# Two side steps later: where TensorE turns the outputs of the recurrence during the first attention

## The chip, the cores and the metric

The kernel runs on one core of a Trainium2 chip. The metric is the device time of one execution in microseconds. Beside the runs that were only timed, one execution was recorded by the hardware profiler; all rows below are from it. Its engines are TensorE (PE; PEld is its weight load), VectorE (DVE), ScalarE (ACT), GpSimd (POOL) and SyncE (SP), which issues nearly all transfers.

## The reference, cut to what matters

A decoder of two layers works on 16 sequences of 128 tokens with 256 channels. In the first layer a causal attention with 16 heads is followed by a recurrence over the tokens, whose keys are the normalised residual and whose values are a context; its outputs are added to the residual, and a mixture of experts follows.

```python
x = x + _L0_attn_ref(_layernorm(x), W_Q, W_K, W_V, W_O, ...)
x = x + _L0_xattn_ref(16, 128, 256, time_decay, time_first, _layernorm(x), ctx_2048)
x = x + _L0_ffn_ref(_layernorm(x), router_w, ...)

# the recurrence, for each of 128 tokens
ww = u + kt
q = maximum(pp, ww)
e1, e2 = exp(pp - q), exp(ww - q)
y_t = (e1 * aa + e2 * vt) / (e1 * bb + e2)
```

## The kernel before, in words

Every engine has a program of its own, written out in Python, and the engines meet at semaphores only. An engine works through its instructions in order, so an instruction that waits holds all that is queued behind it on that engine.

The first attention is a loop of 64 steps `n`. Four steps make a stage `p` (one group `g` of four sequences and four heads), so a group takes 16 steps. In a step TensorE issues the scores (L732), turns the probabilities of two steps ago (L740), does three projections for the next stage (`fill`: six matmuls at L563 to L565 each, to bank 0 and bank 1 by turns), multiplies with the output weights (L759) and with the values (L749). VectorE takes the projected values out of their bank (L1625), copies the attention's output (L1646), adds to the residual (L1653), normalises probabilities (L1641), masks scores (L1631) and takes their maximum (L1634). A projection may not write bank 0 or bank 1 before the one that wrote it last has been taken out; for the values that is L1625.

While the attention of group `g` runs, the recurrence of group `g - 1` and the routing for it are woven in as side work. Side work is a Python generator, of which the loop runs one piece at each `side.step()`. TensorE has five such places in a step `n`: behind the scores, behind L740, behind the first projection, behind the second and behind the third. A `pause(k)` lets k of them go by. So the pauses alone decide between which instructions of the attention a piece of the side work stands.

The recurrence is done in two chunks for each group, `kt` 0 and 1, of 128 channels. For a chunk TensorE turns the normalised tiles into bank 5 (L575), ScalarE copies them out as keys, VectorE does the recurrence with scans (L1294 to L1332) with help of ScalarE and of GpSimd (L2648, L2649), TensorE turns the outputs `w_y` into bank 5 (L608, in `wkv_chunk`), and VectorE adds them to the residual (L1337). Bank 5 is the only bank of the side work: whoever writes it waits on `side_read` until the last content has been read. Six chunks, two each in groups 0 to 2, go through this function; the last group has one of its own (`last_group`).

GpSimd meanwhile splits the weights of the next stages in two parts (L2640, L2642). Each such split waits until the projections that read the old weights have been done.

Of the kernel before, what the change touches and what calls it, by code (L numbers as in the profile page):

```python
# [157 lines left out]
def pause(n):  # L158
    for _ in range(n):
        yield  # L160
# [30 lines left out]
def build(nc, io, out, phases=6):  # L191
    with ExitStack() as ctx:
# [365 lines left out]
        def tensor_program(pe):  # L558
# [13 lines left out]
            def turn_norm(i, kt, to):  # L572
                for b in range(GB):
                    pe.wait_ge(ln_norm, GB * i + b + 1)
                    m = T.transpose(to[:, b * P:(b + 1) * P], tiles_xn[i % 2][:, b, kt * P:(kt + 1) * P], ident[:, :])  # L575
                return m
# [22 lines left out]
            def wkv_chunk(c):  # L599
                g, kt = divmod(c, KT)  # L600
                use = SIDE["key", c]
                pe.wait_ge(side_read, use)
                turn_norm(NORM["wkv", g], kt, bank[5]).then_inc(side_filled, 1)
                yield from pause(15)
                pe.wait_ge(wkv_y, c + 1)
                pe.wait_ge(side_read, SIDE["y", c])
                for b in range(GB):
                    m = T.transpose(bank[5][:, b * P:(b + 1) * P], w_y[:, b, :], ident[:, :])  # L608
                m.then_inc(side_filled, 1)
                yield from pause(2)  # L610

            def wkv_group(g):
                yield from pause(5)
                for kt in range(KT):
                    yield from wkv_chunk(KT * g + kt)
# [2512 lines left out]
```

## Time and profile before

| What | Value |
|---|---|
| Median of 3 runs | 1897.95 us (1893.75 to 1899.11) |
| The profiled execution: its time | 1894.33 us |
| The profiled execution: its span | 1892.5 us |
| TensorE matmul busy | 1639.5 us, 87% of the span |
| VectorE busy | 1256.6 us, 66% |
| ScalarE busy | 877.7 us, 46% |
| GpSimd busy | 549.8 us, 29% |
| The six turns of outputs (L608) | from 247.3 us to 615.4 us |

The shares are averages over stages with different limits. What counts for one edit is the stretch around it: which instruction waits there, for whom, and who waits behind it.

### The profile page before, as it was taken

Reading aid. Unit: us, or ns where it says so; the run is one execution under the profiler, and the core shown is the slowest. Engines: PE = TensorE matmul, PEld = TensorE weight load, DVE = VectorE, ACT = ScalarE, POOL = GpSimd, SP = SyncE. Lnnn points to the kernel's source line nnn. Section 1 sums busy time; section 2 is a strip of 40 time slices with the busy share of each in tenths; the row PEclk is TensorE's granted clock in tenths of the full one; section 3 lists DMA queues with packets and bytes.
Section 4 is the critical chain, followed back from the end, with each engine's and each line's share of the span. In section 5 each row is a group of like instructions: output and inputs, shape, how many; then the busy total and the mean of one; then the engine's idle time right before and its main releaser. Section 6 shows DMA issues by size and latency. Waiting matters only on the chain. (4 is left out here: it accounts for less than half of the span.)

```text
span 1892.5 us, 25681 instructions
## 1 busy us (share of the span) xinstructions
PE 1639.5 (87%) x8566; PEld 1307.3 (69%) x8566; DVE 1256.6 (66%) x2677; ACT 877.7 (46%) x2528; POOL 549.8 (29%) x443
## 2 busy tenths in 40 slices
PE   6999979988997877799997688799878999999866
PEld 5878868776876655577775366577657887788644
DVE  4654786777688666454445556765656778877878
ACT  4534434434443444122222334555336666666666
POOL 2132331723352163300005654552123122211000
PEclk9999999988999898899998678899899999999989
DMA  7243433422352062233334110000100111000001
GB/s 262 68 137 120 160 99 112 169 95 95 130 190 98 28 178 68 73 106 106 107 93 141 34 34 23 23 1 1 45 24 28 39 41 41 12 1 1 1 1 45
DMA packets 82072, 143.37 MB, mean 76 GB/s; under 512 B 8981, under 2 KB 44437, under 8 KB 81813
## 3 DMA queue, kind: packets, MB, share of 16 engines
q1 hardware_dynamic: 75796, 124.94, 20.3%
q0 software_dynamic: 6144, 16.79, 2.7%
q8 instruction: 70, 1.15, 0.3%
q14 instruction: 62, 0.50, 0.1%
HBM read 86.90 MB, written 54.79 MB: 75 GB/s over the span
## 5 line engine op out<-in xcount | busy, mean ns | idle before, releaser
L2308 ACT ACTIVATE self_attention<-self_attention,small 128x128 f32<-128x128 f32 x256 | 99.9, 392 | 121.8 <-DVE small L1634 121.8
L2838 POOL TENSOR_TENSOR cross_attention_heads<-cross_attention_heads 128x512 f32<-128x512 f32 x64 | 70.4, 1100 | 285.2 <-DVE cross_attention_heads L1977 285.2
L2453 ACT ACTIVATE narrow_attention<-bank,small 128x128 f32<-128x128 f32 x256 | 90.4, 365 | 110.7 <-DVE small L1867 110.4
L759 PE MATMUL bank<-self_attention 128*128 128x256 f32 x512 | 130.4, 400 | 12.8 <-DVE residual L1653 12.8
L2537 ACT ACTIVATE cross_attention_heads<-cross_attention_heads,small 128x128 f32<-128x128 f32 x256 | 99.6, 390 | 90.2 <-DVE small L2001 90.2
L1103 PE MATMUL bank<-cross_attention,cross_attention_heads 128*128 128x256 f32 x512 | 124.8, 387 | 15.0 <-DVE residual L2015 10.1
L2704 POOL DMA_INDIRECT narrow_attention<-picked_outputs,dispatch x64 | 62.8, 981 | 235.4 <-DMA picked_outputs<-tiles 207.4
L563 PE MATMUL bank<-x_channel_major,qkv_weights_split 128*128 128x512 f32 x256 | 118.0, 461 | 6.6 <-DVE qkv_weights_split L1671 2.9
L759 PEld LDWEIGHTS bank<-self_attention 128*128 128x128 f32 x512 | 101.0, 201 | 32.3 <-DVE residual L1653 16.4
L1103 PEld LDWEIGHTS bank<-cross_attention,cross_attention_heads 128*128 128x128 f32 x512 | 95.5, 191 | 38.3 <-DVE residual L2015 22.3
L2640 POOL CAST qkv_weights_split<-self_attention 128x1024 fp32r<-128x1024 f32 x45 | 49.5, 1100 | 249.2 <-DMA self_attention<-in_wqkv 195.0
L2642 POOL TENSOR_TENSOR qkv_weights_split<-self_attention,qkv_weights_split 128x1024 fp32r<-128x1024 f32 x45 | 107.8, 2395 | 3.6
L857 PE MATMUL bank<-experts,tiles 128*128 x316 | 108.7, 467 | 0.0
L2316 ACT COPY self_attention<-bank 128x512 f32<-128x512 f32 x64 | 37.5, 585 | 143.2 <-PE bank L740 143.2
L564 PE MATMUL bank<-x_channel_major,qkv_weights_split 128*128 128x512 f32 x256 | 102.8, 401 | 0.0
L565 PE MATMUL bank<-x_channel_major,qkv_weights_split 128*128 128x512 f32 x256 | 102.5, 400 | 0.0
L1625 DVE TENSOR_TENSOR self_attention<-bank,self_attention 128x512 f32<-128x512 f32 x64 | 43.7, 684 | 84.8 <-PE bank L565 84.6
L959 PE MATMUL bank<-narrow_attention 128*128 128x16 f32 x512 | 70.2, 270 | 25.2 <-DVE narrow_attention L1872 14.2
L959 PEld LDWEIGHTS bank<-narrow_attention 128*128 128x128 f32 x512 | 69.5, 211 | 29.0 <-DVE narrow_attention L1872 28.6
L575 PE MATMUL bank<-identity,normalised_tiles 128*128 128x128 f32 x160 | 36.8, 337 | 58.9 <-DVE normalised_tiles L1237 35.6
L1077 PEld LDWEIGHTS bank<-cross_attention,cross_attention_heads 128*128 128x128 f32 x512 | 66.7, 192 | 27.0 <-issue 26.8
L1765 DVE TENSOR_TENSOR experts<-experts,bank 128x176 f32<-128x176 f32 x79 | 26.6, 337 | 87.1 <-ACT experts L2409 87.1
(382 smaller groups left out, 4735.6 us busy)
## 6 DMA issues: line engine op xcount, KB each, us to landing
picked_inputs<-self_attention SPq DMA_DIRECT2D x64, 512.0 KB, 6.2
self_attention<-in_wqkv SPq DMA_DIRECT2D x48, 512.0 KB, 6.1
experts_far<-picked_inputs SPq DMA_DIRECT2D x79, 128.0 KB, 2.0
picked_outputs<-tiles SPq DMA_DIRECT2D x79, 128.0 KB, 1.7
self_attention<-in_wo SPq DMA_DIRECT2D x16, 512.0 KB, 4.1
experts<-in_moe SPq DMA_DIRECT2D x4, 1408.0 KB, 13.8
self_attention<-in_bv SPq DMA_DIRECT2D x16, 256.0 KB, 5.3
bitnet_weights<-in_bitgu SPq DMA_DIRECT2D x8, 416.0 KB, 3.3
```

The source lines that it names most:

```text
L563: T.matmul(out_ap, w_hi, x_hi, start=first, stop=False)
L564: T.matmul(out_ap, w_hi, x_lo, start=False, stop=False)
L565: return T.matmul(out_ap, w_lo, x_hi, start=False, stop=last)
L759: m = T.matmul(bank[7][:, 0:D], ZT_a[n % 2][:, h, :], wo_a[p % 2][:, h, :], start=h == 0, stop=h == HG - 1)
L857: m = T.matmul(bank[2 + n % 2][:, 0:2 * EI].rearrange("p (m c) -> p m c", m=2), t_xT[n % 2][:, k, :], wup[:, :, k, bass.ds(at, EI)], start ...
L959: m = T.matmul(bank[6][:, hh * DS:(hh + 1) * DS], n_PT[n % 2][:, h, :], n_v[bb % 8][:, hh * DS:(hh + 1) * DS], start=True, stop=True)
L1103: m = T.matmul(bank[7][:, 0:D], ZT_x[n % 2][:, h, :], x_wo[hg % 2][:, h, :], start=h == 0, stop=h == HG - 1)
L2308: m = S.activation(P_a[u][:, h, :], P_a[u][:, h, :], ACT.Exp, bias=negmax_a[u][:, h:h + 1], accum_out=sums_a[u][:, h:h + 1])
L2453: m = S.activation(n_P[v][:, h, :], s4_in[:, h, :], ACT.Exp, bias=n_negmax[v][:, h:h + 1], accum_out=n_sums[bb % 2][:, q4 * 4 + h:q4 * 4 + ...
L2537: m = S.activation(P_x[u][:, h, :], P_x[u][:, h, :], ACT.Exp, bias=negmax_x[u][:, h:h + 1], accum_out=sums_x[u][:, h:h + 1])
L2642: G.tensor_tensor(wqkv[m][1], third(t), wqkv[m][0].bitcast(F32), ALU.subtract).then_inc(w_split, 1)
L2838: G.tensor_tensor(x_qsq, x_queries[f % 2], x_queries[f % 2], ALU.mult).then_inc(x_squared, 1)
```

## The change

The pause ahead of the turn of the outputs grows from 15 to 17 side steps, and the pause of two behind it goes. The steps of a chunk add up to the same number, so all that comes after keeps its place. No instruction is added or removed, and the other engines' programs are the same.

```diff
                 turn_norm(NORM["wkv", g], kt, bank[5]).then_inc(side_filled, 1)
-                yield from pause(15)
+                yield from pause(17)
                 pe.wait_ge(wkv_y, c + 1)
                 pe.wait_ge(side_read, SIDE["y", c])
                 for b in range(GB):
                     m = T.transpose(bank[5][:, b * P:(b + 1) * P], w_y[:, b, :], ident[:, :])
                 m.then_inc(side_filled, 1)
-                yield from pause(2)
+                yield from pause(0)
```

Two places on TensorE show it. The first is the first chunk of a group (`kt` 0). Before, the turn of the outputs (L608) stood between the scores and the turn of the probabilities:

```order
L732 MATMUL bank2<-self_attention 128x128 x4
L608 MATMUL bank5<-identity,wkv 128x128 x4
L740 MATMUL bank4<-identity,self_attention 128x128 x4
L563 MATMUL bank0<-x_channel_major,qkv_weights_split 128x512
L564 MATMUL bank0<-x_channel_major,qkv_weights_split 128x512
L565 MATMUL bank0<-x_channel_major,qkv_weights_split 128x512
L563 MATMUL bank0<-x_channel_major,qkv_weights_split 128x512
L564 MATMUL bank0<-x_channel_major,qkv_weights_split 128x512
L565 MATMUL bank0<-x_channel_major,qkv_weights_split 128x512
L575 MATMUL bank5<-identity,normalised_tiles 128x128 x4
```

Now it stands behind L740 and one projection, right ahead of the turn of the second chunk's keys (L575):

```order
L732 MATMUL bank2<-self_attention 128x128 x4
L740 MATMUL bank4<-identity,self_attention 128x128 x4
L563 MATMUL bank0<-x_channel_major,qkv_weights_split 128x512
L564 MATMUL bank0<-x_channel_major,qkv_weights_split 128x512
L565 MATMUL bank0<-x_channel_major,qkv_weights_split 128x512
L563 MATMUL bank0<-x_channel_major,qkv_weights_split 128x512
L564 MATMUL bank0<-x_channel_major,qkv_weights_split 128x512
L565 MATMUL bank0<-x_channel_major,qkv_weights_split 128x512
L608 MATMUL bank5<-identity,wkv 128x128 x4
L575 MATMUL bank5<-identity,normalised_tiles 128x128 x4
```

L608 writes bank 5 and L575 writes it again, so L575 waits for L1337, which reads it in between; nothing is left on TensorE to do between the two.

The second place is the second chunk of a group (`kt` 1), in the last step of a stage. Before, L608 stood behind the second projection of the step, the one to bank 1, and ahead of L759:

```order
L565 MATMUL bank1<-qkv_weights_split,x_channel_major 128x512
L608 MATMUL bank5<-identity,wkv 128x128 x4
L759 MATMUL bank7<-self_attention 128x256 x4
L563 MATMUL bank0<-qkv_weights_split,x_channel_major 128x512
L564 MATMUL bank0<-qkv_weights_split,x_channel_major 128x512
```

Now L759, the projection to bank 0, L749 and the last projection of the step, again to bank 1, all stand ahead of it:

```order
L565 MATMUL bank0<-qkv_weights_split,x_channel_major 128x512
L749 MATMUL bank6<-self_attention 128x128 x4
L563 MATMUL bank1<-qkv_weights_split,x_channel_major 128x512
L564 MATMUL bank1<-qkv_weights_split,x_channel_major 128x512
L565 MATMUL bank1<-qkv_weights_split,x_channel_major 128x512
L563 MATMUL bank1<-qkv_weights_split,x_channel_major 128x512
L564 MATMUL bank1<-qkv_weights_split,x_channel_major 128x512
L565 MATMUL bank1<-qkv_weights_split,x_channel_major 128x512
L608 MATMUL bank5<-identity,wkv 128x128 x4
L732 MATMUL bank2<-self_attention 128x128 x4
```

So L759, two projections of six matmuls each, and L749 pass L608.

## Rows read from the trace of the kernel before

**Rows 1.** Who waited for whom: engine, line, releaser; us, times, longest.

```profile
PE bank L608 <- DVE wkv L1332: 22.8, 3, 8.6
```

**Rows 2.** Timeline around the first chunk: start, duration, engine, instruction, idle before.

```profile
243.08 0.79 PE L563 MATMUL bank<-qkv_weights_split,x_channel_major 128*128 128x512 f32 x1 [4.90 <-DVE self_attention L1625]
...
245.80 1.91 PE L732 MATMUL bank<-self_attention 128*128 128x128 f32 x8
247.50 1.01 PE L608 MATMUL bank<-identity,wkv 128*128 128x128 f32 x4
...
252.14 0.66 PE L575 MATMUL bank<-identity,normalised_tiles 128*128 128x128 f32 x4 [1.79 <-DVE residual L1337]
```

**Rows 3.** Timeline of VectorE in the first group: add of chunk 0, then chunk 1.

```profile
251.41 0.68 DVE L1337 TENSOR_TENSOR residual<-bank,residual 128x512 f32<-128x512 f32 x1
...
280.77 0.41 DVE L1653 TENSOR_TENSOR residual<-bank,residual 128x256 f32<-128x256 f32 x1
...
286.20 0.68 DVE L1625 TENSOR_TENSOR self_attention<-bank,self_attention 128x512 f32<-128x512 f32 x1
287.48 0.69 DVE L1337 TENSOR_TENSOR residual<-bank,residual 128x512 f32<-128x512 f32 x1 [0.61 <-PE bank L608]
291.56 0.69 DVE L1625 TENSOR_TENSOR self_attention<-bank,self_attention 128x512 f32<-128x512 f32 x1 [3.39 <-PE bank L565]
...
295.60 2.39 DVE L1641 TENSOR_TENSOR self_attention<-self_attention,small 128x512 f32<-128x512 f32 x1
```

**Rows 4.** Timeline of VectorE at the second chunks of the groups after it.

```profile
445.82 0.41 DVE L1653 TENSOR_TENSOR residual<-bank,residual 128x256 f32<-128x256 f32 x1
...
451.24 0.68 DVE L1625 TENSOR_TENSOR self_attention<-bank,self_attention 128x512 f32<-128x512 f32 x1
...
457.68 0.69 DVE L1625 TENSOR_TENSOR self_attention<-bank,self_attention 128x512 f32<-128x512 f32 x1 [4.47 <-PE bank L565]
...
611.51 0.41 DVE L1653 TENSOR_TENSOR residual<-bank,residual 128x256 f32<-128x256 f32 x1
...
621.25 0.69 DVE L1625 TENSOR_TENSOR self_attention<-bank,self_attention 128x512 f32<-128x512 f32 x1 [4.70 <-PE bank L565]
```

**Rows 5.** Timeline of TensorE at the same two places.

```profile
451.38 1.11 PE L608 MATMUL bank<-identity,wkv 128*128 128x128 f32 x4 [8.58 <-DVE wkv L1332]
452.28 3.62 PE L759 MATMUL bank<-self_attention 128*128 128x256 f32 x8
...
458.29 0.48 PE L563 MATMUL bank<-qkv_weights_split,x_channel_major 128*128 128x512 f32 x1
...
459.76 1.05 PE L732 MATMUL bank<-self_attention 128*128 128x128 f32 x8
...
614.72 1.11 PE L608 MATMUL bank<-identity,wkv 128*128 128x128 f32 x4 [5.58 <-DVE wkv L1332]
615.62 3.62 PE L759 MATMUL bank<-self_attention 128*128 128x256 f32 x8
...
623.32 1.05 PE L732 MATMUL bank<-self_attention 128*128 128x128 f32 x8
```

**Rows 6.** Timeline of TensorE in the first group, after the second chunk.

```profile
296.38 1.89 PE L759 MATMUL bank<-self_attention 128*128 128x256 f32 x8
...
300.86 0.50 PE L563 MATMUL bank<-x_channel_major,qkv_weights_split 128*128 128x512 f32 x1 [0.31 <-ACT self_attention L2298]
```

**Rows 7.** Timeline of GpSimd there.

```profile
293.94 1.04 POOL L2640 CAST qkv_weights_split<-self_attention 128x1024 fp32r<-128x1024 f32 x1 [8.21 <-PE bank L565]
295.06 2.38 POOL L2642 TENSOR_TENSOR qkv_weights_split<-self_attention,qkv_weights_split 128x1024 fp32r<-128x1024 f32 x1
```

**Rows 8.** Two lines' instructions: duration ns min/median/max, first and last start.

```profile
L1641 DVE TENSOR_TENSOR self_attention<-self_attention,small x64: 691/692/2408, 44.2 to 648.7; 128x512 f32<-128x512 f32 x64
L1220 DVE BATCH_NORM_STATS2 small<-residual x96: 401/409/428, 4.5 to 1822.5; 128x6 f32<-128x256 f32 x96
```

**Rows 9.** Timeline of TensorE in a later stage, after a gap of another length.

```profile
756.40 1.60 PE L821 MATMUL bank<-identity,experts 128*128 128x128 f32 x8 [2.90 <-ACT experts L2388]
```

## The prediction

> **What bounds the kernel now.** I read the list of waits first, then the timelines of TensorE and VectorE around the six turns of the outputs, since the change touches nothing else. TensorE sits idle ahead of L608 in only three of the six chunks: 22.8 us in all, the longest 8.6 [rows 1]. These are the second chunks of the three groups; in the first chunks L608 starts at once behind L732 [rows 2]. The reader should see why those 8.6 us aren't all to be had. L608 waits for VectorE, and VectorE isn't idle while TensorE waits: it works in order through the recurrence and the attention's pieces, and its idle time around L608 is short before L1337 (0.61 us) and long behind it (3.39 us, waiting for a projection) [rows 3]. So in this stretch VectorE leads up to L1337; behind it TensorE leads for a moment, because it has been kept from its projections. What can be saved is what VectorE waits for these projections, less what it will wait for the later L608. The profiled execution took 1894.33 us, span 1892.5; the median of the three runs is 1897.95. I carry the difference over onto the median.
>
> **First chunks (three).** L608 goes behind L740 and a projection. The same instructions lie between L732 and L575, so they end when they ended before, 1.79 us before L575 started, at 250.35 [rows 2]. VectorE comes to L1337 only at 251.41, busy with its queue [rows 3]. L608 is therefore about 1.06 us early even in its new place, L1337 stays where it is, and so does L575 behind it. The other two groups show the same order of events. Cost 0, hidden by VectorE's queue. If that cover went, every microsecond of lateness would count on both engines, since L575 now has nothing ahead of it.
>
> **Second chunks (three).** TensorE no longer stops for the outputs. Next it is held by L759, which needs VectorE's L1653: its end is at 280.77 + 0.41 = 281.18, 445.82 + 0.41 = 446.23 and 611.51 + 0.41 = 611.92 [rows 3, 4]. From L759 to the end of the last projection TensorE took 459.76 - 452.28 = 7.48 us in the second group and 623.32 - 615.62 = 7.70 in the third, both begun after a long gap, at the lower clock (the eight matmuls of L759 took 3.62 us there and 1.89 in a busy stretch) [rows 5, 6]. I take these lengths, for the gap ahead of L759, though shorter, is still long: TensorE fell idle at 451.38 - 8.58 = 442.80 and 614.72 - 5.58 = 609.14 [rows 5], so 3.5 and 2.8 us. Inside the stretch the last projection needs bank 1, which L1625 frees at 286.20 + 0.68 = 286.88 and 451.24 + 0.68 = 451.92 [rows 3, 4]. It would start 7.48 - (459.76 - 458.29) = 6.01 us in, at 287.2 and 452.3, so this adds nothing. Then comes L608 at the full clock (0.66 us, the length of L575, four turns of the same size [rows 2]), then L1337 (0.69), then the L1625 that VectorE waited for before. With 0.03 us for the start of L759:
> - first group: 281.21 + 7.48 + 0.66 + 0.69 = 290.04, where it was 291.56: 1.5 us gained;
> - second: 446.26 + 7.48 + 0.66 + 0.69 = 455.09, was 457.68: 2.6 us;
> - third: 611.95 + 7.70 + 0.66 + 0.69 = 621.00, was 621.25: 0.25 us.
>
> **GpSimd's split.** The split of the weights waits for the last projection. It began at 293.94, as soon as that had ended, and its second half ran from 295.06 to 297.44 [rows 7]; L1641, which started in that time, took 2.39 us, while its median is 0.692 [rows 3, 8]. The last projection now ends at 281.21 + 7.48 = 288.69 instead, 5.25 us earlier, so the second half runs from 289.8 to 292.2, and L1641 comes at 295.60 - 1.52 = 294.1: clear of it, 1.70 us shorter. TensorE can't follow all the way. L759 at 296.38 stood 0.78 us behind L1641's start, up to which it can close; and the projection at 300.86 had 0.31 us idle [rows 6]. So of 1.70 us 1.09 counts. The second group has the same pattern; in the third nothing is left to split. That is 2 x 1.09 = 2.2 us.
>
> Here the Trainium skill has a rule that would turn this term round. What the rows show: L1641 is held, but L1220, the statistics of the normalisation, never is: 96 of them took 401 to 428 ns [rows 8]. In its new place the split runs while VectorE is at L1220. The Trainium skill, SBUF — State Buffer, calls the port pair of VectorE and GpSimd an exclusive lock for which the loser fully blocks, for VectorE's instructions with two SBUF inputs or in a two-port mode. L1641 agrees, and L1220 has a single input; had it such a mode, the split would hold it, and the sum would be that of the third rival. I go by the rows: the sum keeps this term.
>
> **Sum.** 0 + 1.5 + 2.6 + 0.25 + 2.2 = 6.5 us. 1894.3 becomes 1887.8, and on the median 1897.95 - 6.5 = 1891.4. I expect it to reach the end of the kernel, since what follows starts by semaphores, with no fixed time in it.
>
> **Bounds of the clock.** A gap of 2.90 us was followed by slow matmuls (1.60 us for eight turns) and one of 1.79 wasn't (0.66 for four) [rows 9, 2]. The new gap of the third group, 2.8 us, lies by the first, so I take slow. Were TensorE at full clock throughout, L759 to the last projection would take 300.86 - 0.31 - 296.38 = 4.17, and with 1.47 for the projection 5.64 us [rows 5, 6]. The third group would gain 7.70 - 5.64 = 2.1 us more; the first two are then held by L1625 at 286.88 and 451.92 and gain 0.3 each. Best case 6.5 + 2.7 = 9.2 us, or 10.4 if the whole 1.70 counts twice.
>
> **Rivals.**
> 1. *TensorE stays at the lower clock through the whole stretch* (slower). It now has two short gaps in place of one long, and does its work between. At that clock a projection takes 245.80 - 243.08 = 2.72 us, L732 and so L749 1.70, L608 1.01 [rows 2], L759 3.62 [rows 5]: with two projections and L1337 12.46 us from L759 on. That gives 293.7, 458.7 and 624.4, against 291.56, 457.68 and 621.25: 2.1 + 1.0 + 3.2 = 6.3 us lost, 1904.3. It decides where L759 to L608's end passes 291.56 - 281.21 - 0.69 = 9.7 us in the first group, instead of 8.14. Against it: after the single gap the last projection was at full speed, 1.47 us [rows 5].
> 2. *It is taken back later.* TensorE is 87% busy overall; if later pieces are TensorE's or the transfers' to set, an early VectorE only waits longer. Then 1897.95, with an even chance for either side of it. For it speaks that VectorE waited 3.39 and 4.47 us for projections [rows 3, 4]; against, that behind the chunk TensorE itself waits for VectorE and ScalarE [rows 6].
> 3. *The split moves onto L1220.* L1220 would stand still from about 290.7 to 292.2, 1.5 us in each of two groups. The sum would be 6.5 - 3.0 = 3.5 us, 1894.5. Its steady length speaks against it [rows 8].
> 4. *Full clock early*: 9.2 us, 1888.7.
>
> **How the numbers follow.** Forecast (gain of 4.5 to 8.5 us) 0.50, rival 4 0.12, rival 3 0.10, rival 2 0.20, rival 1 0.08. 0.3%, about what a measurement tells from no change, is 5.7 us. Of the forecast's half some two thirds lie above it (0.35), rival 4 too (0.12), and a little of the others: faster 0.50. Rival 1 lies just past the bound on the other side, partly: slower 0.07. Same 0.43. The range reaches from rival 4 with the full 1.70 us and a little (1886.5) to no change (1898); the forecast's own is 1889 to 1893.5.
>
> **What would show it.** In the changed kernel's trace: no wait of TensorE for L1332 any more; gaps of about 3.5, 3.5 and 2.8 us ahead of L759 for L1653 instead; L1337 in second chunks waiting 2 to 5 us for L608; the L1625 behind it without a wait; L1641 behind it at 0.69 us in all three groups; in first chunks L575 with the same gap of 1.8 to 2.4 us. Wrong it would be if the wait ahead of L575 grew past 2.5 us, if L1337's wait reached 6 us, or if from 320 us on the trace ran no earlier than now.

## The result, and the profile after

| Kernel | Median of 8 runs | Ratio, 95% interval |
|---|---|---|
| before | 1896.16 us (1893.75 to 1899.11) | |
| changed | 1886.33 us (1880.97 to 1887.58) | 0.9945, 0.9933 to 0.9957 |

By the ratio the change takes 10.4 us off, 8.2 to 12.7 by its interval. Forecast were 1891.4 us, a gain of 6.5, and a range down to 1886.5. It is faster, by more than the forecast, and its median lies 0.2 us past the end of the range. Part of that is the starting point: the prediction started from 1897.95, the median of three runs, and the median of eight runs of the same kernel is 1896.16, 1.8 us lower. The execution that was profiled took 1886.36 us, with a span of 1884.5.

The list of waits of the changed kernel (us, times, longest), against [rows 1]:

```profile
PE bank L759 <- DVE residual L1653: 26.6, 13, 3.9
...
DVE residual L1337 <- PE bank L608: 8.8, 3, 4.5
...
PE bank L575 <- DVE residual L1337: 5.6, 3, 2.0
```

L608 has left the list. TensorE's idle time has moved to L759 (12.8 us in the kernel before), and VectorE now waits for the turn of the outputs ahead of L1337 for 8.8 us (1.8 us before). Whether that is a gain can't be read from this list, only from the timelines. First TensorE:

```profile
252.10 0.60 PE L608 MATMUL bank<-identity,wkv 128*128 128x128 f32 x4
...
254.61 0.66 PE L575 MATMUL bank<-identity,normalised_tiles 128*128 128x128 f32 x4 [1.91 <-DVE residual L1337]
...
283.70 2.85 PE L759 MATMUL bank<-self_attention 128*128 128x256 f32 x8 [3.49 <-DVE residual L1653]
...
290.91 0.60 PE L608 MATMUL bank<-identity,wkv 128*128 128x128 f32 x4
...
296.12 1.99 PE L759 MATMUL bank<-self_attention 128*128 128x256 f32 x8 [1.50 <-DVE residual L1653]
...
447.11 2.43 PE L759 MATMUL bank<-self_attention 128*128 128x256 f32 x8 [3.50 <-DVE residual L1653]
...
454.34 0.60 PE L608 MATMUL bank<-identity,wkv 128*128 128x128 f32 x4
...
607.54 2.43 PE L759 MATMUL bank<-self_attention 128*128 128x256 f32 x8 [2.84 <-DVE residual L1653]
...
614.64 0.60 PE L608 MATMUL bank<-identity,wkv 128*128 128x128 f32 x4
...
619.85 3.78 PE L759 MATMUL bank<-self_attention 128*128 128x256 f32 x8 [3.28 <-DVE residual L1653]
```

Then VectorE, first chunk and second chunk of the first group, and the L1337 of the other two groups:

```profile
253.88 0.68 DVE L1337 TENSOR_TENSOR residual<-bank,residual 128x512 f32<-128x512 f32 x1
...
285.51 0.69 DVE L1634 TENSOR_REDUCE small<-self_attention 128x4 f32<-128x512 f32 x1
...
291.55 0.69 DVE L1337 TENSOR_TENSOR residual<-bank,residual 128x512 f32<-128x512 f32 x1 [2.18 <-PE bank L608]
292.16 0.68 DVE L1625 TENSOR_TENSOR self_attention<-bank,self_attention 128x512 f32<-128x512 f32 x1
292.75 1.40 DVE L1220 BATCH_NORM_STATS2 small<-residual 128x6 f32<-128x256 f32 x4
...
296.19 0.69 DVE L1641 TENSOR_TENSOR self_attention<-self_attention,small 128x512 f32<-128x512 f32 x1
...
303.90 0.69 DVE L1634 TENSOR_REDUCE small<-self_attention 128x4 f32<-128x512 f32 x1
...
454.98 0.69 DVE L1337 TENSOR_TENSOR residual<-bank,residual 128x512 f32<-128x512 f32 x1 [2.19 <-PE bank L608]
...
615.28 0.69 DVE L1337 TENSOR_TENSOR residual<-bank,residual 128x512 f32<-128x512 f32 x1 [4.46 <-PE bank L608]
```

And GpSimd's split beside it:

```profile
291.21 1.04 POOL L2640 CAST qkv_weights_split<-self_attention 128x1024 fp32r<-128x1024 f32 x1 [3.00 <-PE bank L565]
292.33 2.39 POOL L2642 TENSOR_TENSOR qkv_weights_split<-self_attention,qkv_weights_split 128x1024 fp32r<-128x1024 f32 x1
```

These rows show most steps of the mechanism as forecast. The gaps ahead of L759 are 3.49, 3.50 and 2.84 us (forecast 3.5, 3.5, 2.8). From L759 to L608 TensorE took 7.21, 7.23 and 7.10 us (7.48, 7.48, 7.70). L1337 waits 2.18, 2.19 and 4.46 us (2 to 5). The L1625 behind it waits for nothing. L1641 is at 0.69 us where it had 2.39 [rows 3]. L575 has a gap of 1.91 us, against 1.79 [rows 2]. The absolute times of the two profiles aren't compared here: this one was already 2.04 us later at the first L1634 of the kernel (39.19 against 37.15 us), far ahead of the first changed instruction. For the same reason the prediction's last sign of being wrong can't be read from absolute times: counting steps from 0, the L1634 of step 29 began at 303.90 us here and at 304.61 before, that of step 43 at 448.92 and 448.08. I compare lengths.

**A measure that one profile can give.** VectorE runs L1634 once in each step of the attention; the steps are counted from 0. From the start of it in step 27 to that in step 29 spans the second chunk of the first group: 303.90 - 285.51 = 18.39 us above. Steps 43 to 45 and 59 to 61 do the same for the other groups. The experiments below are read by these three lengths beside their times.

### The profile page after: what moved, and what is told of

Read it like the earlier page. It is cut to its first block and busy times, and to the rows that moved or that the text cites. A ratio compares the mean times of both kernels' runs of the same rounds, so it can differ in the third digit from the quotient of the medians.

```text
span 1884.5 us, 25681 instructions
## 1 busy us (share of the span) xinstructions
PE 1639.8 (87%) x8566; PEld 1307.6 (69%) x8566; DVE 1251.3 (66%) x2677; ACT 877.3 (47%) x2528; POOL 551.0 (29%) x443
## 5 line engine op out<-in xcount | busy, mean ns | idle before, releaser
L759 PE MATMUL bank<-self_attention 128*128 128x256 f32 x512 | 128.9, 397 | 26.6 <-DVE residual L1653 26.6
L759 PEld LDWEIGHTS bank<-self_attention 128*128 128x128 f32 x512 | 99.2, 197 | 46.5 <-DVE residual L1653 31.4
L2642 POOL TENSOR_TENSOR qkv_weights_split<-self_attention,qkv_weights_split 128x1024 fp32r<-128x1024 f32 x45 | 108.0, 2399 | 3.6
L1625 DVE TENSOR_TENSOR self_attention<-bank,self_attention 128x512 f32<-128x512 f32 x64 | 43.7, 684 | 74.6 <-PE bank L565 74.5
L575 PE MATMUL bank<-identity,normalised_tiles 128*128 128x128 f32 x160 | 36.5, 335 | 57.4 <-DVE normalised_tiles L1237 34.8
```

What stands on the lines that cost most here:

```text
L759: m = T.matmul(bank[7][:, 0:D], ZT_a[n % 2][:, h, :], wo_a[p % 2][:, h, :], start=h == 0, stop=h == HG - 1)
L2642: G.tensor_tensor(wqkv[m][1], third(t), wqkv[m][0].bitcast(F32), ALU.subtract).then_inc(w_split, 1)
```

## The experiments

Seventeen further runs were made, four of them of a kernel that had been run already. Those made together form a set and shared the runs of the kernel before, and its level differed: medians of 1896.16 to 1896.39 in three sets, the first result's among them, and 1904.37 to 1905.95 in the other three. So every time is read as the ratio to its own set. Each length is from one profile. The three lengths, us:

| Kernel | step 27 to 29 | 43 to 45 | 59 to 61 | sum | ratio, 95% interval |
|---|---|---|---|---|---|
| before | 21.56 | 22.65 | 17.87 | 62.08 | |
| `before_again` | 22.91 | 22.95 | 18.00 | 63.86 | 1.0005, 0.9996 to 1.0013 |
| `first_only` | 22.87 | 20.96 | 16.48 | 60.31 | 1.0000, 0.9984 to 1.0017 |
| `split_late` | 22.30 | 21.12 | 17.88 | 61.30 | 0.9984, 0.9972 to 0.9996 |
| `before_warm` | 22.84 | 21.71 | 15.15 | 59.70 | 0.9984, 0.9968 to 1.0000 |
| `before_gap_filled` | 20.17 | 20.18 | 15.15 | 55.50 | 0.9984, 0.9966 to 1.0003 |
| `gap_filled_2` | 20.19 | 20.17 | 15.16 | 55.52 | 0.9978, 0.9962 to 0.9994 |
| changed | 18.39 | 18.42 | 18.91 | 55.72 | 0.9945, 0.9933 to 0.9957 |
| `after_again` | 18.40 | 19.23 | 15.34 | 52.97 | 0.9957, 0.9939 to 0.9975 |
| `after_third` | 18.40 | 17.30 | 18.91 | 54.61 | 0.9944, 0.9920 to 0.9968 |
| `second_only` | 18.39 | 18.40 | 18.91 | 55.70 | 0.9942, 0.9919 to 0.9966 |
| `first_late` | 18.39 | 18.39 | 18.94 | 55.72 | 0.9961, 0.9946 to 0.9976 |
| `split_collides` | 19.75 | 19.75 | 18.90 | 58.40 | 0.9954, 0.9939 to 0.9969 |
| `warm` | 18.40 | 18.40 | 16.36 | 53.16 | 0.9954, 0.9938 to 0.9969 |
| `one_step` | 17.61 | 17.05 | 13.07 | 47.73 | 0.9914, 0.9884 to 0.9944 |
| `second_one_step` | 17.05 | 17.05 | 13.07 | 47.17 | 0.9918, 0.9898 to 0.9938 |
| `one_step_warm` | 17.04 | 17.06 | 13.08 | 47.18 | 0.9909, 0.9890 to 0.9928 |
| `one_step_split` | 16.50 | 15.39 | 13.07 | 44.96 | 0.9898, 0.9878 to 0.9917 |
| `all_three` | 18.06 | 16.50 | 13.07 | 47.63 | 0.9934, 0.9916 to 0.9951 |

### The two halves of the change

Only the first chunks, `first_only`:

```diff
-                yield from pause(15)
+                yield from pause(15 if kt else 17)
...
-                yield from pause(2)
+                yield from pause(2 if kt else 0)
```

> Pauses 17 and 0 in first chunks only. My account: no change, within 1.5 us of the kernel before; L1337 is reached by VectorE about 1 us after L608 has ended. Rival (the turn right ahead of L575 lengthens TensorE's wait): 1 to 3 us slower.

Only the second chunks, `second_only`, with `if kt` the other way round:

```diff
-                yield from pause(15)
+                yield from pause(17 if kt else 15)
...
-                yield from pause(2)
+                yield from pause(0 if kt else 2)
```

> Pauses 17 and 0 in second chunks only, 15 and 2 in first chunks. My account: first chunks are covered by the queue of VectorE, so the whole gain stays: 9 to 11 us under the kernel before. Rival (L740 and a projection coming earlier in first chunks helps too): a gain smaller by 1 us or more than that of the full change.

And both kernels once more, with no edit but an empty line at the end:

> The changed kernel once more, unaltered, for a second profile. In the first one the gain behind the last second chunk came in jumps: 2 us lost where L759 began at the lower clock at 619.85, 2.6 us won where another L759 did not at 651.85. If these jumps are the clock's chance, they stand elsewhere in this profile and the median stays 9 to 11 us under that of the kernel before; the DVE gains of the second chunks (3.2, 4.2 and 0.9 us) come again within 0.5 us. If they belong to the change, the same instructions are slow again.

> The kernel before once more, unaltered. In the first profile TensorE met the end of the attention and the opening of the experts with slow matmuls that no changed kernel shows, the one with first chunks alone included: 2 to 3.6 us between 644 and 731 us. If that is the clock's chance, this profile does not show it, and the steps from the 28th to the 30th maximum (L1634) of the stage differ by up to 1.7 us from the first profile. Time the same within 0.15%.

Within the intervals the first chunks are worth nothing (1.0000), the second chunks everything (0.9942, the changed kernel beside it 0.9957). The kernel before, run again, gave 1.0005.

The two repeats also tell where the first group's forecast was short. VectorE in `before_again`, at the three L1625 for which the prediction had read 3.39, 4.47 and 4.70 us [rows 3, 4]:

```profile
286.42 0.69 DVE L1634 TENSOR_REDUCE small<-self_attention 128x4 f32<-128x512 f32 x1
...
296.28 0.69 DVE L1625 TENSOR_TENSOR self_attention<-bank,self_attention 128x512 f32<-128x512 f32 x1 [4.73 <-PE bank L565]
...
309.33 0.69 DVE L1634 TENSOR_REDUCE small<-self_attention 128x4 f32<-128x512 f32 x1
...
463.49 0.69 DVE L1625 TENSOR_TENSOR self_attention<-bank,self_attention 128x512 f32<-128x512 f32 x1 [4.78 <-PE bank L565]
...
627.31 0.69 DVE L1625 TENSOR_TENSOR self_attention<-bank,self_attention 128x512 f32<-128x512 f32 x1 [4.81 <-PE bank L565]
```

All three wait 4.7 to 4.8 us. TensorE's L759 in the first group, in the kernel before and then in `before_again`, shows where the difference comes from:

```profile
287.24 2.91 PE L759 MATMUL bank<-self_attention 128*128 128x256 f32 x8
```

```profile
290.61 3.62 PE L759 MATMUL bank<-self_attention 128*128 128x256 f32 x8
```

Behind gaps of 8.59 and 9.05 us both begin at the lower clock, and the first returns to the full one sooner. So the 3.39 us was one execution's value, and the prediction had taken it for the place's own. By it the first length of the kernel before is 1.35 us shorter than in `before_again` (21.56 against 22.91). It isn't the only low one: the same wait is 3.89 and 3.29 us in the second and third groups of `first_only`.

### The cover of the first chunks

`first_late` is the changed kernel with 18 turns of the identity, results unused, ahead of L608 in first chunks:

```diff
                 yield from pause(17)
+                if not kt:
+                    pe.wait_ge(side_read, SIDE["y", c])
+                    for _ in range(18):
+                        T.transpose(bank[5][:, 0:P], ident[:, :], ident[:, :])
                 pe.wait_ge(wkv_y, c + 1)
```

> The changed kernel, with 18 turns of the identity ahead of L608 in first chunks, 2.1 us of work on TensorE. My account says that L608 is covered there for about 1.1 us, VectorE coming to L1337 no sooner: 1 us lost in each of three groups, 3 us slower than the changed kernel. Rival (there is no slack at all, or bank 5 is on the path): 6 us slower. Rival (TensorE has ample slack): same as the changed kernel.

(In this kernel the turn of the outputs is L612 and L1337 is L1341.) TensorE and VectorE there:

```profile
249.63 2.13 PE L608 MATMUL bank<-identity 128*128 128x128 f32 x18
...
252.98 0.66 PE L575 MATMUL bank<-identity,normalised_tiles 128*128 128x128 f32 x4 [0.79 <-DVE residual L1341]
...
252.23 0.69 DVE L1341 TENSOR_TENSOR residual<-bank,residual 128x512 f32<-128x512 f32 x1 [0.20 <-PE bank L612]
```

Started 1.97 us later, the turn makes VectorE wait 0.20 us here, and 1.07 and 0.82 in the other groups. So VectorE's queue covered 1.8, 0.9 and 1.1 us of lateness, about the forecast's 1.06. Whether what lies past that costs time is not shown: the ratio is 0.9961 beside the change's 0.9945, and the intervals overlap.

### GpSimd's split

`split_collides` is the changed kernel with the split held back until VectorE has done the statistics, which puts its second half beside L1641 again:

```diff
+                    if p in (7, 11):
+                        pool.wait_ge(ln_stats, NORM["routing", p // NHG - 1] + 1)
                     split_wqkv(p + 1, 2)
```

> The changed kernel, in which the same split is held until the statistics (L1224) behind the second chunk are done, so that it runs beside L1641 as in the kernel before. My account: 2 to 3.4 us slower than the changed kernel, that is 6 to 8 us under the kernel before, L1641 at 2.4 us again. Rival (the split has no part in the gain): the gain stays at 9 to 10 us.

`split_late` is the kernel before with the split held until past that L1641:

```diff
+                    if p in (7, 11):
+                        pool.wait_ge(a_probs, GB * p)
                     split_wqkv(p + 1, 2)
```

> The kernel before, in which GpSimd's split of the last third of the weights waits, in the two stages behind a second chunk, until L1641 has ended (one more wait, no other edit). My account says that L1641 held by the split costs 1.1 to 1.7 us in each of two groups: 2 to 3.4 us under the kernel before, L1641 at 0.69 us. Rival (the split's overlap costs nothing, TensorE sets the pace there): no change.

VectorE in `split_collides`:

```profile
296.54 2.45 DVE L1641 TENSOR_TENSOR self_attention<-self_attention,small 128x512 f32<-128x512 f32 x1
...
459.89 2.45 DVE L1641 TENSOR_TENSOR self_attention<-self_attention,small 128x512 f32<-128x512 f32 x1
```

The collision is back, 2.45 against 0.69 us, and the two stretches grew from 18.39 and 18.42 to 19.75 and 19.75: 1.3 to 1.4 us of the 1.76 count in each. The forecast had 1.09. In `split_late` both L1641 took 0.69 us, and it gained 3.0 us (0.9984). By the lengths it is less there: from the L1625 that VectorE waits for to the end of the length it is 13.05 us in the kernel before and 12.49 in `split_late`, in both groups, so holding the split back gives 1.1 us in all in the old order. So the term is real, 2.7 us instead of 2.2 by the lengths in the changed order; the time of `split_collides` (0.9954) is too close to the changed kernel's for the medians to tell. The row of L1220 above (four in 1.40 us) ran wholly beside L2642 (292.33 to 294.72) at its usual length. With that the third rival falls. This trace agrees with the rule of the Trainium skill, SBUF — State Buffer, section "SBUF: two separate sides", as the prediction read it: L1641, VectorE's instruction with two SBUF inputs, is held (2.45 us), and L1220 isn't.

### The clock

By the lengths, the lower clock behind the long gap is the dearest thing in the stretch, and it differs from profile to profile. `before_warm` is the kernel before with 40 idle turns in the gap, `before_gap_filled` and `gap_filled_2` (one kernel, run twice) with as many as fill it, `warm` the changed kernel with 20 in its own gap:

```diff
                 yield from pause(15)
+                if kt:
+                    pe.wait_ge(side_read, SIDE["y", c])
+                    for _ in range(74 if g < 2 else 46):
+                        T.transpose(bank[5][:, 0:P], ident[:, :], ident[:, :])
                 pe.wait_ge(wkv_y, c + 1)
```

(`range(40)` in `before_warm`; in `warm` `range(20)`, and a `pause(2)` behind it.)

> The kernel before, with 40 turns of the identity into bank 5, read by nobody, ahead of L608 in second chunks, so that TensorE works through 4.7 us of the gaps of 8.6 and 5.6 us. It undoes only the lower clock behind the gap; the order stays. If that clock is what made VectorE wait for its projection 3.4 us in one profile and up to 4.8 in others, the wait falls to about 2.3 us each time: 3 to 7 us under the kernel before. If the gain of the change comes from the order alone, it is the same as the kernel before.

> The changed kernel with 20 turns of the identity into bank 5, which nobody reads, at the place where L608 stood in second chunks, so that TensorE works in the gap ahead of L759. If the lower clock behind that gap costs what the rows say, L759 takes 1.9 us instead of 2.4 to 2.9, L608 ends 0.3 us sooner in two groups and 1.6 sooner in the third, and the slow L759 at 619.85 (3.78 us) is gone: 1 to 4 us under the changed kernel. Rival (the gap is covered, VectorE sets the pace): same as the changed kernel. If the turns take longer than the gap of 2.8 us, they push L759 back instead.

> The kernel before, with 74 turns of the identity (46 in the third group) ahead of L608 in second chunks, 8.4 and 5.2 us of work in gaps of 8.6 and 5.6 us. With 40 turns a gap of 4.2 us was left in two groups and L608 was slow again there; only the third group was served, whose wait of VectorE fell from 4.7 to 2.4 us. If the clock is the larger part of what the change saves, all three waits are about 2.4 us now, and the time is 5 to 8 us under the kernel before. If the order is, 2 us at most.

> The kernel before with its gaps filled, once more. Its trace had the three steps around second chunks 6.6 us shorter in all than the kernel before, as short as in the changed kernel, but its time was only 3 us less, on a chip on which a transfer came late in every profile. If the late transfers hid the rest, it is 5 to 8 us under the kernel before here; if the 3 us are the truth, the shorter steps are given back elsewhere.

TensorE and VectorE in `gap_filled_2`, where the real turn is L612, L759 is L763 and L1625 is L1629:

```profile
279.12 8.24 PE L608 MATMUL bank<-identity 128*128 128x128 f32 x74
287.93 0.65 PE L612 MATMUL bank<-identity,wkv 128*128 128x128 f32 x4 [0.57 <-DVE wkv L1336]
288.42 1.89 PE L763 MATMUL bank<-self_attention 128*128 128x256 f32 x8
...
291.74 0.69 DVE L1629 TENSOR_TENSOR self_attention<-bank,self_attention 128x512 f32<-128x512 f32 x1 [2.43 <-PE bank L565]
```

With TensorE busy through the gap the granted clock stays full (1.00 from 288.42 to 290.30 us, where it was 0.50 from 452.28 to 455.50 in the kernel before). The eight matmuls of L759 take 1.89 us instead of 3.62 [rows 5], and VectorE's wait for the projection shrinks from 4.7 to 2.4 us. The order is the one of before; still the three lengths fall from 62.08 us to 55.5. So in these lengths the old order has two costs: some 6.6 us for the clock, and a rest for the order. What the change gives at full clock is seen from `warm`: 53.16, that is 2.3 us less than 55.5. That rest is no more than the split's 2.7 us: L1641 took 2.39 us in `gap_filled_2`, as in the kernel before, and 0.69 us in `warm`.

`warm` shows one thing more. In its first group TensorE has

```profile
285.20 1.99 PE L764 MATMUL bank<-self_attention 128*128 128x256 f32 x8 [1.30 <-DVE residual L1658]
...
292.41 0.60 PE L613 MATMUL bank<-identity,wkv 128*128 128x128 f32 x4
```

From L759 (L764 here) to the turn (L613 here) it is 7.21 us at full clock too, as in the changed kernel with L759 at 2.85 us, and the first two lengths are the same 18.4 us. The last projection waits there for its bank, which L1625 frees: in the changed kernel at 288.69 + 0.68 = 289.37 us, 5.67 us behind the start of L759. With 1.47 us for the projection that makes 7.1 of the 7.2 us. The forecast for `warm` is missed accordingly: its time is not below the changed kernel's (0.9954 against 0.9945), though its third length is 2.55 us shorter.

The 40 turns of `before_warm` didn't reach far enough. They took 4.53 us and left a gap of 4.24 us, and L612 was at the lower clock again (1.12 us for four turns, against 0.66); in the third group the gap left was 1.22 us, and there the clock held:

```profile
279.99 4.53 PE L608 MATMUL bank<-identity 128*128 128x128 f32 x40
...
288.76 1.12 PE L612 MATMUL bank<-identity,wkv 128*128 128x128 f32 x4 [4.24 <-DVE wkv L1336]
...
617.50 0.66 PE L612 MATMUL bank<-identity,wkv 128*128 128x128 f32 x4 [1.22 <-DVE wkv L1336]
```

Here time and trace part. The filled kernels gained 3.0 and 4.2 us by their ratios, not 6.6, and the interval of the first reaches 1.0003. `after_third`, the changed kernel unaltered, ran beside `gap_filled_2` to settle this:

> The changed kernel beside it on the same chip. 8 to 11 us under the kernel before; its three steps at 53 to 56 us together. If the clock behind the gap is most of what the change saves, it is at most 5 us under gap_filled_2.

It gained 10.7 us (0.9944), where the filled gap gained 4.2, though by the three lengths the two differ by one microsecond only. So the difference lies elsewhere. One thing sets these profiles apart. In all nine runs of the sets at 1904 us or more, and in none of the other eight nor in the first profiles of the kernel before and the changed one, the steps 34 and 50 take 12 to 17 us instead of 9.6, with waits such as this one of `after_again`, which names no instruction of the kernel:

```profile
ACT self_attention L2316 <- remote: 19.0, 2, 9.6
```

From the L1634 of step 29 to that of step 43 and from 45 to 59 it is together 286.1 us in the kernel before, 284.3 in `after_third`, 292.4 in `gap_filled_2` and 299.6 in `before_gap_filled`. That is 8.1 us between the two that ran beside each other, where their gains differ by 6.5. It doesn't settle the matter. Only 2.5 of the 8.1 us lie in steps 34 and 50 themselves, the rest is spread over the other steps; kernels without such waits range from 285.7 to 290.5 us as well; and the two profiled executions are 12.0 us apart (1885.61 and 1897.63 us), twice what the medians are. I don't know what these waits are: the expectation of `gap_filled_2` speaks of late transfers, and no row shows that. Nor do I know why the filled kernels would be longer here. How the 10.4 us divide between order and clock in time thus stays open; the lengths of the trace divide theirs, 7.3 (worked out below), into 2.3 for the order with the split, and 5.0 for the clock.

### One step later instead of two

In `one_step` L608 stands behind L759 and one projection; L749 and the last projection come after it:

```diff
-                yield from pause(15)
+                yield from pause(16)
...
-                yield from pause(2)
+                yield from pause(1)
```

`second_one_step` has this in second chunks only. `one_step_warm` adds the 20 turns of `warm` in second chunks, `one_step_split` the wait of `split_late`, and `all_three` has both.

> Pauses 16 and 1: L608 one side step later than before. In second chunks it stands behind L759 and the projection to bank 0, ahead of L749 and the last projection. My account, from the rows of the changed kernel: L1337 no longer waits 2.2 us, so the L1625 behind it comes some 2 us sooner; but the split then runs beside L1641 again and gives 0.5 to 1 us of it back in two groups. Some 1 to 4 us under the changed kernel. Rival (L608 later is better because TensorE has less to do behind it): 2 to 6 us slower than the changed kernel.

> One side step later in second chunks only; first chunks as in the kernel before. Since first chunks did nothing in either direction, it is as fast as one step later in both: 13 to 18 us under the kernel before.

> One step later in both chunks, and 20 turns of the identity in second chunks in the gap ahead of L759. The trace of one step later has L759 at the lower clock in two groups (3.78 and 2.68 us); at the full clock L608 would wait for L1332 instead, which ends about 0.6 us before L608 now starts: 0 to 2 us under one step later. If it is slower than that, the turns stand in the way of L759.

> One step later, and GpSimd's split held until L1641 has ended in the two stages behind a second chunk. In the trace of one step later L1641 took 1.79 us there, 1.1 more than its 0.69. If VectorE sets the pace behind the chunk, 1 to 2 us under one step later; if TensorE does, the same as it.

> One step later, 20 turns of the identity in the gap ahead of L759 in second chunks, and the split held until L1641 has ended. One step later gave 16 us, the turns up to 2 more, the held split 1 to 3: 17 to 21 us under the kernel before. If the two helpers serve the same wait, it is no faster than one_step_split.

TensorE and VectorE in `one_step`:

```profile
282.60 3.78 PE L759 MATMUL bank<-self_attention 128*128 128x256 f32 x8 [3.50 <-DVE residual L1653]
...
288.34 0.60 PE L608 MATMUL bank<-identity,wkv 128*128 128x128 f32 x4
...
288.97 0.69 DVE L1337 TENSOR_TENSOR residual<-bank,residual 128x512 f32<-128x512 f32 x1 [0.71 <-PE bank L608]
...
293.61 1.79 DVE L1641 TENSOR_TENSOR self_attention<-self_attention,small 128x512 f32<-128x512 f32 x1
...
613.95 0.69 DVE L1337 TENSOR_TENSOR residual<-bank,residual 128x512 f32<-128x512 f32 x1 [0.58 <-PE bank L608]
```

L608 comes soon enough that L1337 waits 0.7 us at most instead of 2.18 to 4.46, and one projection still overtakes it. The third group, 18.91 us in the changed kernel, takes 13.07. L1641 is held again for 1.1 us, and `one_step_split` takes that away. The ratios are 0.9914, 0.9918, 0.9909 and 0.9898: 16 to 19 us off the kernel before, the last the lowest ratio measured here. These four lie below every kernel with two steps, whose ratios are 0.9942 to 0.9961; beside one another in one set were `one_step` and the unaltered changed kernel, 0.9914 and 0.9957, with intervals that just touch; `second_only`, in the same set, has 0.9942. That puts `one_step` 5 to 8 us under the kernels with two steps, where 1 to 4 had been expected. The order among the four is not shown. `all_three` is worse than its parts (0.9934); it has 293.3 us from step 29 to 43 and 45 to 59, where `one_step_split` of another set has 287.8, so much of it lies in those same steps, cause open. `all_three` had been forecast at 17 to 21 us and gained 12.6. `one_step_warm` shows no gain clear of the others either (0.9909).

## Why the prediction was right in direction and short in size

The median came out 5.1 us under the forecast of 1891.4 us, and 1.8 us of that is the starting point. The rest is the gain: by the ratio it is 10.4 us, 3.9 more than the 6.5 forecast. The mechanism held in the main; what failed is the sizing of three terms:
- the first group's 1.5 us, 1.45 too small, since one profile's 291.56 was taken as the place's value;
- the third group's 0.25 us, which stops at its L1625 and leaves out the gap behind it; by the lengths it is a loss;
- what lies outside the three stretches, put at nothing ("I expect it to reach the end"), where 3.1 us of the 10.4 lie.

Rows explain the first two. The cause of the third is open.

**First chunks, 0.** Right: `first_only` 1.0000, and the cover of 1.06 us confirmed by `first_late`.

**Second chunks, 1.5 + 2.6 + 0.25 = 4.35 us.** Mis-sized. The profiles with the order of before in second chunks (before, `before_again`, `first_only`) have mean lengths of 22.45, 22.19 and 17.45 us, those with the changed order (changed, `after_again`, `after_third`, `second_only`) 18.40, 18.34 and 18.02. The differences are 4.05, 3.85 and -0.57 us, together 7.3, in which the split's term is contained. With that term the forecast had 2.6, 3.7 and 0.25, together 6.5. These are means of three and four profiles; single lengths of one order differ by up to 3.6 us.
- *First group*, 1.45 us too low: its 291.56 came from an execution in which VectorE waited 3.39 us, while `before_again` has 4.73. What failed is "where it was 291.56", one profile's row taken as the place's value; its neighbour of 4.47 us [rows 4] stood beside it as a warning.
- *Second group*: 3.85 for 3.7. In both groups the prediction let the clock set the 7.48 us from L759 on and said that the wait for bank 1 adds nothing. It was the other way round: L1625 set the 7.2 us (`warm`, above). Only where L759 took the whole 3.78 us, in the second group of `after_again`, did the clock set it, 8.04 us. The error is 0.3 us in each.
- *Third group*: a small loss for a small gain. L1625 was indeed reached in time, but the prediction stopped there. The next L759 (619.85) has a gap of 3.28 us, which was 0.41 before, and took 3.78 us, the granted clock of that stretch being 0.50:

```profile
619.85:623.40 3.55, 3.55 (x8) 2.85 (x9) 3.37 (x9) 1.99 (x8) 0.00 (x0) 0.50 0.02 8
```

(A window of the trace: its stretch and length, then busy time and instructions of TensorE, weight loads, VectorE, ScalarE and GpSimd, the granted clock, share and rate of the transfers.) `after_third` and `second_only` show the same 3.78. In `after_again` it took 1.99 us behind the same gap, and the L759 one step earlier, behind 2.85 us of idle, had kept the full clock as well (1.99 us at 610.90, against 2.43). That alone doesn't decide it: in `warm` that L759 took 1.99 us too, and the one behind 3.28 us of idle 3.10. The third length is 15.34, not 18.91:

```profile
621.59 1.99 PE L759 MATMUL bank<-self_attention 128*128 128x256 f32 x8 [3.28 <-DVE residual L1653]
```

**GpSimd's split, 2.2 us.** Right, 2.7 by the lengths of `split_collides`.

**"I expect it to reach the end."** It did, and some more. From the last L1634 of this attention to the second statistics behind it (L1220, at 731.51 us in the kernel before) the kernel before, `before_again` and `first_only` took 86.98, 87.07 and 83.31 us, mean 85.8, the four with the new order 83.8. That is 2.0 us, for which the prediction had no term. The row that makes most of it is the second L759 in this tail. In `first_only`, `before_again` and the changed kernel, in this order, it is

```profile
659.92 1.99 PE L759 MATMUL bank<-self_attention 128*128 128x256 f32 x8 [1.50 <-DVE residual L1653]
```

```profile
661.33 3.78 PE L759 MATMUL bank<-self_attention 128*128 128x256 f32 x8 [1.66 <-DVE residual L1653]
```

```profile
651.85 1.99 PE L759 MATMUL bank<-self_attention 128*128 128x256 f32 x8 [1.47 <-DVE residual L1653]
```

The same matmuls take 1.99 or 3.78 us there. The old order doesn't bring the slow ones by itself: besides `first_only`, `split_late` and `before_warm` have 84.83 and 84.75 us in all and 1.99 us in this row. Whether the change has a part in it or chance isn't settled, and the 2.0 us is more likely too large than too small. 7.3 + 2.0 = 9.3 us lies inside the measured 8.2 to 12.7. In the first two profiles alone the account closes: 6.4 us in the three stretches and 3.5 in this tail, of 10.0 us from the first L1634 to the end.

**Bounds of the clock.** The best case there, 9.2 to 10.4 us, is where the result lies, but by another road. It was to come from full clock behind the gap; TensorE began at the lower clock there in all three groups (L759 took 2.85, 2.43 and 2.43 us), as forecast. Only its smaller part came true, L1625 setting the pace in the first two groups for 0.3 us each. The rest of the surplus that is explained came from the kernel before being worse than its one profile.

**The rivals.** Rival 1, the lower clock through the whole stretch, fell: L608 took 0.60 us each time, at full clock, and from the start of L759 to the end of L608 it was 7.7 to 7.8 us, under the forecast's 8.14 and far from the 9.7 at which it decides. Rival 2, taken back later, fell by the ratio, and rival 3 by L1220's row. Rival 4 gave nearly the right number, and most of its mechanism didn't happen.

## What to carry to other kernels

An instruction that waits in an in-order queue may be sunk past independent work, but only so far as its own reader allows: here one step later was worth some 16 us and two some 10. At two steps VectorE waited 2 to 4.5 us in each of three places for the turn, at one step 0.7 us at most. Ask for both ends, what the waiting instruction holds up and who waits for it.

Behind idle gaps of TensorE, a stretch of one profile carries the clock that this execution was granted, 1.4 us in one place here and 3.6 in another; the same place in the other groups, or a second profile, shows how much. Work out too what the next instruction waits for at either clock: in the first group here it was a bank, and L759 at 1.99 or at 2.85 us made no difference. And a wait that disappears at one line leaves a gap one step on, whose clock has to be priced too.

## What was not expected of the hardware

- The same gap was followed by different clocks: behind 3.28 us of idle L759 took 3.78 us in three profiles and 1.99 in one, of programs alike in this stretch. In two further kernels it took 3.78 and 3.79, and in `warm` 3.10.
- Useless matmuls paid: 74 turns of the identity in 8.24 us of waiting shortened each of the first two stretches by some 2 us. In time the two runs gained 3.0 and 4.2 us, and the interval of the first includes no gain.
- One and the same program, the kernel before, stood at 1896 or at 1905 us in different sets. With the slower level came two steps of 12 to 17 us, among waits that name no instruction of the kernel. Their cause wasn't found.
